# An attention and mixture-of-experts kernel whose setup is re-sorted around one batch, with later row sends and changed tail, projection and masks

## The chip, the cores and the metric

One core of a Trainium2 chip runs the whole kernel. The metric is device time in microseconds of one execution; lower is better.

## The reference

The input x is (8 batches, 512 tokens, 128). It is normalised over its last axis (xn), and two branches read xn. The first is causal attention with 32 query heads, 16 key and value heads of 64, an ALiBi bias, and an output projection. The second is a mixture of 8 experts: a gate chooses the best two of eight for each token, each expert is 128 to 512 to 128 with an exact GELU. The result is x plus attention times silu of the mixture.

```
qkv = xn @ W_qkv
scores = q @ k.T / 8 + slope[h] * (j - i);  causal;  softmax;  @ v;  @ W_out
gate_logits = xn @ gate_w + gate_b;  top 2;  softmax over the two
y[e] = gelu(xn @ w1[e] + b1[e]) @ w2[e] + b2[e];  weighted sum over the two
out = x + s * silu(ffn)
```

## The kernel before

All matrix work is done in fp16 pairs: a number is held as a high and a low half, and a product is three matmuls (`three`). The attention is cut into 64 **bodies**, each one pair of key and value heads (two slots) of one batch. A body consists of named steps: K, Q, V projections, M (rough scores, whose row peaks DVE takes as B), C (turned shifts), S (scores, ten groups), E (exponentials on ScalarE), L (low halves on POOL), P (values), N (normalise), A (output halves, moved through a transposing DMA), O (output projection, accumulated into `att` by DVE). `ORDER` writes out by hand, for each engine, the steps of one **window** in a fixed order; an entry such as `("R0", 2, 0)` is step R0 of the body two ahead of the window, at place 0 in per cent of the window. Engines run their lists strictly in order. Each half of the bodies has entering windows (before its first body), a loop over windows in pairs, some windows written out at either end, and leaving windows.

Around them: a **setup** (load x, statistics on DVE, normalised tiles in `mix`, turned by TensorE into `xT_hi` and `xT_lo`; weights split into halves; gate logits; the choice of two experts; ranks of the tokens; routing, which gives each token a slot in `slot_x`). Then the first half of the bodies. During it ScalarE (R), POOL (I, D) send each tile's rows to their slots with indirect DMAs, two transfers for each of 32 tiles, and the expert weights are loaded and split (W). Then the expert blocks. Then the second half, in which expert outputs are fetched and added into `mix` (F, G). Then the **tail**: silu, multiply, add x, write out.

Before the change the setup handles all eight batches at each step, the choice stands before the first projections, and POOL waits for the routing before it starts its windows. Row t is sent in step with body t. In a score group each part ends with its own mask matmul of 67 columns (line 887). The project step waits for both slots and goes through four token tiles with both slots inside. The tail is one silu over 4096 columns, four pieces of 1024 columns multiplied on DVE, and two of them added on POOL and two on DVE.

## Time and profile before

| what | us |
|---|---|
| median of three runs | 1264.25 (1263.28 to 1268.05) |
| profiled execution | 1263.92 |
| its span | 1262.0 |
| PE busy | 1154.3 (91%) |
| DVE busy | 1015.8 (80%) |
| ACT busy | 935.5 (74%) |
| POOL busy | 879.9 (70%) |

PE is TensorE, DVE VectorE, ACT ScalarE, POOL GpSimd. The span counts from the first to the last record of the profiled execution; 1.9 us lie around it. PE's matmuls are pipelined and their ends are modelled, so the distance between the starts of two of them says more than their lengths.

### The profile page before, as it was taken

To read this page: it belongs to the slowest core of one execution; us is meant where nothing else is said; L and a number is where in the kernel's file an instruction comes from. 1 tells how busy PE (TensorE), PEld (TensorE's weight loads), DVE (VectorE), ACT (ScalarE), POOL (GpSimd) and SP (SyncE) were. 2 spreads that over 40 slices of the span, in tenths; PEclk is the share of its full clock that TensorE was granted. 3 is DMA by queue.
4 is the path that set the end of the run, shared out by engine and by line. 5 is a ranking of instruction groups with operands and counts; after the bars stand their busy time and mean duration, and the time that the engine had idled before them with its cause. 6 is when DMAs were issued, how large, how long until landed. Compare 5 with 4: busy or idle time off the path is not lost.

```text
span 1262.0 us, 54043 instructions
## 1 busy us (share of the span) xinstructions
PE 1154.3 (91%) x17610; PEld 915.0 (73%) x17610; DVE 1015.8 (80%) x3107; ACT 935.5 (74%) x1790; POOL 879.9 (70%) x1088
## 2 busy tenths in 40 slices
PE   1449999999999999998999789999999999999992
PEld 0327777777777777787888658777777777777782
DVE  8758888888888888885777668888888888888874
ACT  1328888888888888886666468888888888888882
POOL 9128888888888888884000068888888888888883
PEclk9669999999999999999999989999999999999996
DMA  6416666666666666674333366665555555555553
GB/s 211 171 38 134 142 140 148 143 142 144 144 142 144 144 142 144 145 141 93 86 89 82 99 156 137 136 137 133 133 133 133 133 133 133 133 133 133 133 116 84
DMA packets 286165, 165.10 MB, mean 131 GB/s; under 512 B 175011, under 2 KB 274691, under 8 KB 285445
## 3 DMA queue, kind: packets, MB, share of 16 engines
q1 hardware_dynamic: 281988, 155.63, 53.9%
q0 software_dynamic: 4096, 8.40, 2.3%
q8 instruction: 51, 0.84, 0.3%
q14 instruction: 30, 0.24, 0.1%
HBM read 15.76 MB, written 16.78 MB: 26 GB/s over the span
## 4 chain that ended last, share of the span: by engine, by line
PE 78%; DVE 6%; DMA 4%; issue 4%; ACT 3%; SPq 2%; POOL 2%; ACTq 0%; POOLq 0%; DVEq 0%
PE ps L880 10%; PE ps L854 10%; PE ps L782 8%; PE ps L783 7%; PE ps L784 7%; PE ps L884 6%; PE outs L911 6%; PE outs L915 5%; PE outs L913 5%; PE ps L881 4%; DMA k_st<-stage 3%; PE ps L887 2%; PE ps L863 2%; ACT q_st L1109 2%; PE outs L783 1%
## 5 line engine op out<-in xcount | busy, mean ns | idle before, releaser
L743 POOL TENSOR_TENSOR t_lo<-stage 128x512 f16<-128x512 f32 x640 | 654.6, 1038 | 106.6 <-ACT stage L1120 102.1
L1302 DVE CUSTOM_DVE_ANT_0 stage<-ps,kmask 128x512 bf16<-128x512 f32 (+3 forms) x1024 | 467.1, 488 | 118.8 <-PE ps L854 101.6
L1120 ACT ACTIVATE stage<-ps,slope 128x512 f32<-128x512 f32 (+1 forms) x768 | 455.6, 619 | 120.0 <-PE ps L887 82.1
L880 PE MATMUL ps<-q_st,k_st 128*128 128x256 f16 (+3 forms) x1024 | 305.8, 301 | 10.5 <-ACT stage L1120 6.9
L911 PE MATMUL outs<-v_sp,stage 128*128 128x65 f16 x2560 | 282.1, 194 | 4.3 <-DVE stage L1332 2.8
L913 PE MATMUL outs<-v_sp,stage 128*128 128x64 f16 x2560 | 281.9, 193 | 0.0
L915 PE MATMUL outs<-v_sp,t_lo 128*128 128x65 f16 x2560 | 281.8, 193 | 0.0
L854 PE MATMUL ps<-k_st,stage 128*128 128x512 f16 (+3 forms) x1024 | 251.7, 302 | 12.8 <-DVE spread L1302 5.5
L911 PEld LDWEIGHTS outs<-v_sp,stage 128*128 128x128 bf16 x2560 | 238.4, 98 | 12.2 <-issue 4.4
L913 PEld LDWEIGHTS outs<-v_sp,stage 128*128 128x128 bf16 x2560 | 235.9, 98 | 9.0 <-issue 0.3
L915 PEld LDWEIGHTS outs<-v_sp,t_lo 128*128 128x128 f16 x2560 | 235.9, 98 | 0.0
L881 PE MATMUL ps<-q_st,k_st 128*128 128x128 f16 x1024 | 224.2, 219 | 0.0
L884 PE MATMUL ps<-q_st,k_st 67*128 67x384 f16 (+2 forms) x768 | 211.6, 276 | 0.0
L887 PE MATMUL ps<-late_q,late_k 66*128 66x67 f16 x1024 | 188.0, 195 | 0.0
L1109 ACT CAST q_st<-ps 1x512 f16<-1x512 f32 x256 | 147.6, 577 | 17.9 <-PE ps L863 12.3
L880 PEld LDWEIGHTS ps<-q_st,k_st 128*128 128x128 f16 x1024 | 100.2, 98 | 45.5 <-issue 21.6
L1077 ACT ACTIVATE stage<-ps,qscale 128x512 f16<-128x512 f32 x128 | 88.6, 692 | 48.7 <-PE ps L784 48.5
L704 POOL COPY slot_now<-slot_of 128x1 uint32 (+1 forms) x128 | 23.3, 183 | 141.4 <-DMA slot_y<-stage 141.4
L854 PEld LDWEIGHTS ps<-k_st,stage 128*128 128x128 f16 x1024 | 81.7, 98 | 49.3 <-issue 21.6
L884 PEld LDWEIGHTS ps<-q_st,k_st 67*128 67x128 f16 x768 | 74.9, 97 | 51.5 <-issue 1.6
L881 PEld LDWEIGHTS ps<-q_st,k_st 128*128 128x128 f16 x1024 | 100.3, 98 | 13.2 <-issue 0.9
L887 PEld LDWEIGHTS ps<-late_q,late_k 66*128 66x128 f16 x1024 | 100.8, 98 | 0.0
(199 smaller groups left out, 2731.6 us busy)
## 6 DMA issues: line engine op xcount, KB each, us to landing
k_st<-stage SPq DMA_DIRECT2D x256, 128.0 KB, 2.5
q_st<-stage SPq DMA_DIRECT2D x256, 128.0 KB, 2.4
q_st<-stage SPq DMA_DIRECT2D x256, 64.0 KB, 2.1
k_st<-stage SPq DMA_DIRECT2D x128, 64.0 KB, 2.1
slot_y<-stage SPq DMA_DIRECT2D x40, 128.0 KB, 2.0
X<-in_L_attn_inputs SPq DMA_DIRECT2D x8, 512.0 KB, 6.3
slot_x<-att SPq DMA_DIRECT2D x2, 2048.0 KB, 8.7
wx_raw<-in_L_ffn_w SPq DMA_DIRECT2D x64, 64.0 KB, 1.8
```

Source lines behind the costliest of these rows:

```text
L743: pool.tensor_tensor(t_lo[r], t_p[r], upper(t_p[r]), ALU.subtract).then_inc(s[f"lo{u % NG}"], 1)
L854: mm = pe.matmul(M_ps[h][:, c0:c0 + w], q_raw[sl][:, 0, i * P:(i + 1) * P], k_st[par][sl][:, 2 + h, 0:w], start=True, stop=True)
L880: pe.matmul(d, k[:, 0, at], q[:, 0, seen], start=True, stop=False, skip_group_check=True)
L881: pe.matmul(d[:, 0:P], k[:, 1, at], q[:, 1, at], start=False, stop=True, skip_group_check=True)
L884: pe.matmul(d[:, P:], k[far, 1, at], q[far, 1, (kt + 1) * P:SEQ], start=False, stop=True, skip_group_check=True)
L887: mm = pe.matmul(d[:, LATE:P], late_k[late, :], late_q[late, LATE:P], start=False, stop=True, skip_group_check=True)
L911: pe.matmul(d, p_hi, v[:, with_one], start=(opens and i == kt), stop=False, skip_group_check=True)
L913: pe.matmul(d[:, OUT_COL[sl]:OUT_COL[sl] + DH], p_hi, v[:, lo], start=False, stop=False, skip_group_check=True)
L915: mm = pe.matmul(d, t_lo[r][:, c], v[:, with_one], start=False, stop=(closes and i == QT - 1), skip_group_check=True)
L1109: ins = act.copy(q_st[sl][h][DH:DH + 1, 1, :], M_ps[0][SHIFT[h]:SHIFT[h] + 1, :])
L1120: e = act.activation(t_p[r][:, c0:c1], S_ps[u % 2][:, c0:c1], ACT.Exp, scale=slope[:, bass.ds(pair_index(n) * 2 * SLOTS + sl * 2 + h, 1)])
L1302: ins = dve.tensor_tensor_reduce(junk[h][:, c0:c0 + w], M_ps[h][:, c0:c0 + w], kmask[:, SEQ - w:SEQ], -1.0 / 1024, 3e38, ALU.add, ALU.min, ...
```

## The change

The setup starts with one batch of x, then the K and V weights, then Q, then the rest of x, then W_out (to another place). DVE, ScalarE and TensorE carry batch 0 through to the projections of body 0, with the splits of weights in between, and only then take batches 1 to 7, whose tiles are normalised half by DVE and half by ScalarE (`norm_odd`). POOL makes the mask rows first, and its share of the weight splits is gone. The gate follows, then the entering windows, and the choice of experts is cut into three parts that DVE runs after its steps B1, B3 and B5 of the first entering window (`CHOICE`). The ranks follow the entering windows on TensorE. POOL waits for the routing only before it sends the first row.

Rows are sent with the body two later (`sent_with`), R0 stands at place 72 and not 0 of ScalarE's list, and since 32 rows must still go in the first half, bodies 30 and 31 send two rows each. The loops end one pair of windows earlier, and those windows are written out.

In a score group one matmul masks all parts (its moving operand is repeated, its output lies in two places, 67 columns each). The project step goes slot by slot and waits for a slot just before it. The accumulation multiplies by 1/WS. The tail has three pieces of 14, 14 and 4 tiles, each with its own silu, multiplied and added on POOL, DVE and DVE; the first two start before the last body is complete.

```diff
-            ("R0", 2, 0), ("E0", 0, 4), ("E1", 0, 8), ("C1", 0, 12), ("E2", 0, 20), ("A1", -1, 26), ("E3", 0, 29),
...
+            ("E7", 0, 71), ("R0", 2, 72), ("A0", 0, 76), ("E8", 0, 79), ("W0", 0, 83), ("E9", 0, 89), ("Q0", 2, 94),
...
+                if "Y" in tasks and name in CHOICE:
+                    tasks["Y"](n, 0, CHOICE[name])
+
+
+        CHOICE = {"B1": 0, "B3": 1, "B5": 2}
...
-            start, end = lo + 2 * UNROLL, hi - UNROLL
+            start, end = lo + 2 * UNROLL, hi - 2 * UNROLL
...
+
+        LAST = NT - QT
+        PIECES = [(0, LAST // 2), (LAST // 2, LAST), (LAST, NT)]
+
         def out_chunk(v, c):
 
-            return v[:, 8 * c:8 * c + 8, :].rearrange("p t d -> p (t d)")
+            t0, t1 = PIECES[c]
+            return v[:, t0:t1, :].rearrange("p t d -> p (t d)")
+
+        def finish(eng, c):
+
+
+            need(eng, "silu", c + 1)
+            eng.wait_ge(s["acc"], BODIES if c == 2 else BODIES - PAIRS)
+            eng.wait_ge(s["xend"], 64)
+            a, g, xx = (out_chunk(v, c) for v in (att, mix, X))
+            eng.tensor_tensor(a, a, g, ALU.mult).then_inc(s[f"gated{c}"], 1)
+            eng.wait_ge(s[f"gated{c}"], 1)
+            eng.tensor_tensor(xx, xx, a, ALU.add).then_inc(s[f"fin{c}"], 1)
+
+        def sent_with(n):
+
+
+            if not isinstance(n, int):
+                return [n - UNROLL]
+            return [t for t in range(NT) if min(t + UNROLL, HALF - UNROLL + (t - NT) // 2 + UNROLL) == n]
...
+            inputs(0)
+            for c in (1, 0):
+                sp.dma_start(stage[:, c, :], w_qkv[:, c * CH:(c + 1) * CH]).then_inc(s[f"wq{c}"], 16)
+            for c in range(1, 4):
+                inputs(c)
...
-            sp.wait_ge(s["attz"], 1)
+            sp.wait_ge(s["rows"], ROW_STEPS)
...
-                                       row_now[par][:, 0:D], ALU.subtract).then_inc(s["ready0"], 1)
-                indices(n, k, par)
+                for i, t in enumerate(sent_with(n)):
+                    at = t % UNROLL if isinstance(t, int) else par
+                    if isinstance(t, int) and (t, k) == (0, 0):
+                        pool.wait_ge(s["routed"], 1)
+                        pool.wait_ge(s["zeros"], 16 * ZERO_DMAS)
+                    need(pool, f"sent{at}", t // UNROLL * 32)
+                    if k == 0:
+                        pool.wait_ge(s["rhi"], t + 1)
+                        pool.tensor_tensor(row_now[at][:, D:2 * D], mix[:, bass.ds(t, 1), :].rearrange("p a d -> p (a d)"),
+                                           row_now[at][:, 0:D], ALU.subtract).then_inc(s["ready0"], 1)
+                    indices(t, k, at)
...
+            finish(pool, 0)
...
-                    late = slice(0, P - LATE - 1)
-                    mm = pe.matmul(d[:, LATE:P], late_k[late, :], late_q[late, LATE:P],
-                                   start=False, stop=True, skip_group_check=True)
-                mm.then_inc(s[f"scored{u % NG}"], 1)
+
+                late, first = slice(0, P - LATE - 1), [c0 // P for _, _, c0 in GROUPS[u % NG]]
+                d = S_ps[u % 2].rearrange("p (t c) -> p t c", c=P)[:, first[0]:first[-1] + 1:max(first[-1], 1), LATE:P]
+                pe.matmul(d, late_k[late, :], late_q[late, LATE:P].unsqueeze(1).to_broadcast([P - LATE - 1, len(first), P - LATE]),
+                          start=False, stop=True, skip_group_check=True).then_inc(s[f"scored{u % NG}"], 1)
...
+                bank_free(n, "O0")
                 for sl in range(SLOTS):
                     need(pe, f"ta{sl}", (n + 1) * 16)
-                bank_free(n, "O0")
-                for t in range(QT):
-                    tok = slice(t * P, (t + 1) * P)
-                    for sl in range(SLOTS):
-                        j = bass.ds(pair_index(n) * SLOTS + sl, 1)
+                    j = bass.ds(pair_index(n) * SLOTS + sl, 1)
+                    for t in range(QT):
+                        tok = slice(t * P, (t + 1) * P)
+
                         mm = three(bank_of("O0")[:, tok], aT[par][sl][:, tok],
                                    aT[par][sl][:, (QT + t) * P:(QT + t + 1) * P],
                                    wo_hi[:, j, :].rearrange("p a d -> p (a d)"),
                                    wo_lo[:, j, :].rearrange("p a d -> p (a d)"),
...
+            turn_inputs(0)
+            bodies_of_half[:] = 0, HALF
+            keys(0, 0, 0)
+            vals(0, 0, 0)
+            queries(0, 0, 0)
+            queries(0, 0, 1)
+
+            pe.wait_ge(s["sm"], 80)
+            pe.transpose(ps[4][:, 0:E * FC], b1_in[:, :], ident[0:E * FC, 0:E * FC]).then_inc(s["b1tr"], 1)
+            for q in range(1, NB):
+                if q > 4:
+                    pe.wait_ge(s["xlo"], q - 3)
+                turn_inputs(q)
...
+            enter_bodies("PE", tasks, 0, HALF)
...
             pe.wait_ge(s["picked"], 1)
...
-            enter_bodies("PE", tasks, 0, HALF)
...
+                final = isinstance(n, int) and (n, sl) == (BODIES - 1, 1)
+                if final:
+                    act.wait_ge(s["added"], NT)
+                    for c in range(2):
+                        gates(c)
...
+                if final:
+                    gates(2)
...
+                for t in sent_with(n):
+                    at = t % UNROLL if isinstance(t, int) else par
+                    need(act, f"sent{at}", t // UNROLL * 32)
+                    act.copy(row_now[at][:, 0:D], mix[:, bass.ds(t, 1), :].rearrange("p a d -> p (a d)"))\
+                       .then_inc(s["rhi"], 1)
...
+            roots(0, 0, QT)
+            split_hi(K_PART)
+            split_hi(V_PART)
+            turned_hi(0)
+            split_hi(Q_PART)
+            bodies_of_half[:] = 0, HALF
+
+            act.wait_ge(s["wlo"], V_PART + 1)
+            k_hi_part(0, 0, 0)
+            v_hi_part(0, 0, 0)
             act.wait_ge(s["scales"], HQ)
-            act.wait_ge(s["wloP"], len(ON_POOL))
-            go_ahead("ACT", tasks, 0, HALF)
-            enter_bodies("ACT", {**tasks, "W": weights_hi, "R": send_hi}, 0, HALF)
+            for sl in range(SLOTS):
+                q_hi(0, 0, sl)
+            roots(1, QT, NT)
+            act.wait_ge(s["norm"], 1)
+            norm_odd(1)
+            for q in range(1, NB):
+                if q + 1 < NB:
+                    norm_odd(q + 1)
+                turned_hi(q)
+            split_hi(O_PART)
+            act.wait_ge(s["b1tr"], 1)
+            act.copy(b1T[:, :], ps[4][:, 0:E * FC]).then_inc(s["b1"], 1)
+            enter_bodies("ACT", tasks, 0, HALF)
+            act.wait_ge(s["gap"], 1)
+            act.activation(top[:, 5, :], top[:, 4, :], ACT.Exp).then_inc(s["topexp"], 1)
...
+            def choose(k):
+
+
+                if k == 0:
+                    dve.wait_ge(s["consts"], 9)
+                    dve.wait_ge(s["gate"], 1)
+                    small(dve.scalar_tensor_tensor(out=L, in0=ps[5][:, 0:NT * E].rearrange("p (t e) -> p t e", e=E),
+                                                   scalar=1.0 / WS, in1=gb[:, :].unsqueeze(1).to_broadcast([P, NT, E]),
+                                                   op0=ALU.mult, op1=ALU.add))
+                    pick(L, top[:, 0, :], top[:, 1, :], one1)
+                elif k == 1:
+                    small(dve.scalar_tensor_tensor(out=L2, in0=one1, scalar=-3e38, in1=L, op0=ALU.mult, op1=ALU.add))
+                    pick(L2, top[:, 2, :], top[:, 3, :], one2)
+                else:
+                    dve.tensor_tensor(top[:, 4, :], top[:, 2, :], top[:, 0, :], ALU.subtract).then_inc(s["gap"], 1)
+                    dve.tensor_tensor(chosen[:, 0:NT, :], one1, one2, ALU.add).then_inc(s["picked"], 1)
 
             def peaks(n, _, j):
...
 
+                if isinstance(n, int) and n == BODIES - 1:
+                    finish(dve, 1)
                 dve.wait_ge(s["op"], n + 1)
                 a = att[:, bass.ds(batch_index(n) * QT, QT), :].rearrange("p t d -> p (t d)")
-                dve.tensor_tensor(a, bank_of("O0")[:, :], a, ALU.add).then_inc(s["acc"], 1)
+                dve.scalar_tensor_tensor(out=a, in0=bank_of("O0")[:, :], scalar=1.0 / WS, in1=a, op0=ALU.mult,
+                                         op1=ALU.add).then_inc(s["acc"], 1)
...
+            statistics(0, QT)
+            scales_of(0, 0, QT)
+            norm_tiles(range(QT))
+            split_lo(K_PART)
+            turned_lo(0)
+            split_lo(V_PART)
+            bodies_of_half[:] = 0, HALF
+            statistics(QT, 2 * QT)
+            k_lo_part(0, 0, 0)
+            split_lo(Q_PART)
+            v_lo_part(0, 0, 0)
+            statistics(2 * QT, 4 * QT)
+            q_lo(0, 0, 0)
+            statistics(4 * QT, NT)
+            q_lo(0, 0, 1)
+            scales_of(1, QT, NT)
+            norm_tiles(range(QT, 2 * QT, 2))
+            for q in range(1, NB):
+                if q + 1 < NB:
+                    norm_tiles(range((q + 1) * QT, (q + 2) * QT, 2))
+                if q == 2:
...
+                turned_lo(q)
+            split_lo(O_PART)
...
+            enter_bodies("DVE", {**tasks, "Y": lambda n, _, k: choose(k)}, 0, HALF)
+            dve.wait_ge(s["topexp"], 1)
...
+            finish(dve, 2)
```

## Rows read from the trace of the kernel before

**Rows 1.** Windows: busy us of PE, PEld, DVE, ACT, POOL; granted clock, DMA share, GB/s

```profile
40.00:50.00 10.00, 4.91 (x131) 3.68 (x131) 8.68 (x10) 6.67 (x6) 4.15 (x2) 0.61 0.16 67
103.00:568.00 465.00, 460.93 (x7417) 367.73 (x7414) 400.46 (x1283) 390.23 (x747) 402.20 (x477) 1.00 0.64 144
1222.00:1262.00 40.00, 16.36 (x270) 14.63 (x268) 19.65 (x25) 14.16 (x20) 17.35 (x14) 0.69 0.34 80
```

**Rows 2.** Timeline of all engines, 85 to 92 us: start, length, engine, line, operation

```profile
85.24 0.97 POOL L721 DMA_INDIRECT slot_x<-row_now,slot_now  x1 [0.30 <-issue]
...
87.52 0.30 ACT L1142 CAST row_now<-mix 128x128 f16<-128x128 f32 x1 [11.98 <-DMA slot_x<-row_now,slot_now]
...
88.55 0.37 PE L880 MATMUL ps<-q_st,k_st 128*128 128x256 f16 x1 [4.86 <-ACT stage L1120]
```

**Rows 3.** Timeline of DVE, 0 to 115 us

```profile
10.54 1.65 DVE L1233 BATCH_NORM_STATS2 stats<-X 128x6 f32<-128x128 f32 x8 [0.23 <-DMA X<-in_L_attn_inputs]
...
41.66 2.29 DVE L419 SCALAR_TENSOR_TENSOR wq_lo<-stage,wq_hi 128x2048 f16<-128x2048 f32 x1 [1.12 <-ACT wq_hi L407]
...
45.85 0.41 DVE L1265 SCALAR_TENSOR_TENSOR wx_lo<-outs,gb 128x256 f32<-128x256 f32 x1
...
52.44 0.42 DVE L1285 TENSOR_TENSOR chosen<-wx_lo 128x256 f16<-128x256 f32 x1
...
53.65 0.69 DVE L1317 SCALAR_TENSOR_TENSOR stage<-ps,stage 128x512 f16<-128x512 f32 x1
...
63.98 0.69 DVE L1302 CUSTOM_DVE_ANT_0 stage<-ps,kmask 128x512 bf16<-128x512 f32 x1 [0.25 <-DVE wo_lo L419]
...
75.01 0.29 DVE L1367 TENSOR_TENSOR wx_lo<-outs,wx_lo 128x128 f32<-128x128 f32 x1
...
81.93 0.22 DVE L1399 TENSOR_TENSOR slot_of<-slot_of,slot_bits 128x64 uint32<-128x64 uint32 x1
```

**Rows 4.** Timeline of POOL, 0 to 32 us

```profile
21.49 3.54 POOL L681 MEMSET att<- 128x4096 f32 x1
...
29.55 2.11 POOL L700 TENSOR_TENSOR b_row<-wx_hi,b_row 1x1024 f16<-1x1024 f32 x1
```

**Rows 5.** Windows of the tile normalisation, L1248, alone: DVE busy us and count

```profile
22.00:25.00 3.00, 3.00 (x2) 1.00 0.00 0
31.70:33.00 1.30, 1.30 (x7) 1.00 0.94 403
```

**Rows 6.** Timeline of PE, 59 to 66 us: the matmuls of the ranks

```profile
60.18 3.31 PE L948 MATMUL outs<-chosen,ones 128*128 128x256 f16 x32
```

**Rows 7.** Timeline of all engines, 550 to 555 us, in window 29

```profile
551.72 0.59 ACT L1102 CAST stage<-outs 128x512 f16<-128x512 f32 x1
...
551.91 0.99 POOL L721 DMA_INDIRECT slot_x<-row_now,slot_now  x1 [0.17 <-issue]
...
552.97 0.69 DVE L1332 TENSOR_TENSOR stage<-outs,stage 128x512 f16<-128x512 f32 x1
...
553.11 0.22 PE L881 MATMUL ps<-q_st,k_st 128*128 128x128 f16 x1
...
553.16 0.20 PE L887 MATMUL ps<-late_q,late_k 66*128 66x67 f16 x1
...
553.20 0.38 PE L854 MATMUL ps<-k_st,stage 128*128 128x128 f16 x2
...
554.28 0.19 PE L911 MATMUL outs<-v_sp,stage 128*128 128x65 f16 x1
```

**Rows 8.** Timeline of all engines but PE, the last 25 us

```profile
1239.07 3.62 ACT L1213 ACTIVATE mix<-mix 128x4096 f32<-128x4096 f32 x1
...
1246.67 6.46 POOL L775 TENSOR_TENSOR X<-X,att 128x1024 f32<-128x1024 f32 x2 [12.62 <-DVE att L1443]
...
1250.97 3.25 DVE L1447 TENSOR_TENSOR X<-X,att 128x1024 f32<-128x1024 f32 x1
...
1255.39 1.22 DVE L1447 TENSOR_TENSOR X<-X,att 128x1024 f32<-128x1024 f32 x1
```

More of the change, by code:

```diff
@@ L551, in _ @@
             go_ahead("SP", stacks, 0, HALF)
+            sp.wait_ge(s["attz"], 1)
+            zx = slot_x.rearrange("(p a) d -> p (a d)", p=P)
+            none = att[:, :, :].rearrange("p t d -> p (t d)").bitcast(F16)
+            for c in range(0, ZERO, ZERO_ROW):
+                k = min(ZERO_ROW, ZERO - c)
+                sp.dma_start(zx[:, c:c + k], none[:, 0:k]).then_inc(s["zeros"], 16)
             enter_bodies("SP", {**stacks, "W": load_weights}, 0, HALF)
@@ L770, in _ @@
             leave_bodies("POOL", fetches, HALF, BODIES)
-            pool.wait_ge(s["xend"], 64)
-            for c in range(2):
-                pool.wait_ge(s["gated"], c + 1)
-                xx = out_chunk(X, c)
-                pool.tensor_tensor(xx, xx, out_chunk(att, c), ALU.add).then_inc(s["finP"], 1)
+            finish(pool, 0)
         @block.tensor
@@ L879, in scores @@
                     k, q = k_st[par][sl], q_st[sl][h]
-                    pe.matmul(d, k[:, 0, at], q[:, 0, seen], start=True, stop=False, skip_group_check=True)
+                    pe.matmul(d, k[:, 0, at], q[:, 0, seen], start=(c0 == 0), stop=False, skip_group_check=True)
                     pe.matmul(d[:, 0:P], k[:, 1, at], q[:, 1, at], start=False, stop=True, skip_group_check=True)
```

310 lines of the change are left out of this document (136 added, 174 removed), and 2 rows, old and new, of the table ORDER.

## The prediction, written before the change was run

> **What bounds the kernel now.** I read the busy times by stretch first, to see which stretches are not filled by TensorE. From 103 to 568 us PE is busy 460.93 of 465 us at a granted clock of 1.00, so that stage goes at PE's pace; the 40 us at the end hold only 16.36 us of PE work [rows 1]. The other open place is the start, so I read all engines around the first exponentials next. ScalarE sits idle 11.98 us until a transfer into slot_x lands, copies a row at 87.52, and only then starts the exponentials of body 0; TensorE's third score group, which needs one of them, starts at 88.55 after 4.86 us of idling [rows 2]. What holds that transfer is seen on DVE: the choice of experts from 45.85 to 52.86, the first projections of body 0 from 53.65, its peaks from 63.98, then the routing from 75.01 to 82.15, all in one queue [rows 3]. Everything before 88.55 is a serial prologue, everything after it runs at PE's pace. So moving that moment forward should shift the whole trace, until something in a PE-bound stage takes it back.
>
> **The setup.** It is a re-sorting of queues, so I add up the new queues. DVE first. Statistics of a tile cost 0.2 us (8 in 1.65) and splitting 2048 columns of weights 2.29 us [rows 3]; a 512-column low part 0.69 us [rows 3]. Up to the scales of batches 1 to 7 DVE has 32 statistics 6.6, aggregates about 2.2, two sets of seven short operations about 4.5, four normalised tiles 1.0, the splits of K, V and Q 4.6, five low parts 3.5, and some 1.5 us of waits on weights and on PE (an estimate): 24 us. The old one begins its statistics at about 5 us, so I take 28 to 29 us.
>
> Then come 14 tiles on DVE and 14 on ScalarE. POOL's big memset of att begins at 21.49 and its work on b2 ends at 31.66 [rows 4]; in 22 to 25 us DVE finished two tiles in 3 us, and from 31.7 on seven in 1.3 us [rows 5]. POOL's work is only permuted, so its end stays, and the tiles crawl until about 31.7. After that DVE needs 14 x 0.19 + 7 x 0.69 = 7.5 us, ScalarE somewhat more (two tiles and a 512-column cast per batch, about 1.3 us, 7 batches, of which one or two are done by then): the last low part at about 39.5 us. From 40 to 50 us PE ran 131 matmuls in 4.91 us [rows 1], the gate's 128 and three wide ones of about 0.5; the gate alone then 3.4: 43 us, only 3 us earlier than before.
>
> The gain is behind that. Old: choice 7.0, body 0's projections about 8 us (53 to 61), ranks 3.3, entering the bodies 11.0 (63.98 to 75.01), routing 7.1, first rows sent and waited for 5.4 us. New: entering and choice together, 11.0 + 6.1 - 0.6 (the choice's own 15 operations without the one that stood behind POOL, less what falls into DVE's wait for the shifts) = 16.5, to 60 us; three short operations and the ranks (3.31 us for 32 matmuls [rows 6], only behind the entering windows) to 62.3; routing 7.1 to 69.4; two peaks, the turned shifts, and the third score group at 71. The exponential of the gap needs a table load on ScalarE behind its last queries, at 59.5: hidden by the ranks, and worth 1.5 us if it isn't. The projections of body 0 now lie under the statistics and transfers; body 0's stacking waits for POOL's mask rows, due at 16, still 25 us ahead of use. The old moment is 88.55, so **-17.5 us**; bounds -22 (no crawling, no waits) and -11 (ScalarE paces the batches at 1.8 us and choice and peaks do not overlap). The three transfers that clear slot_x move behind body 0's stacking, are out by 29 us, land by about 42, and the first rows go after 69. TensorE's granted clock falls where the prologue leaves it idle (0.61 in 40 to 50 us [rows 1], so partly at the lower of its two levels), and will again; I count no difference.
>
> **Rows sent two bodies later.** Row t goes with body t+2, at the middle of ScalarE's window and no longer at its head; that removes the 11.98 us wait [rows 2], counted above. In the steady stage the copy (0.3 us) now stands ahead of the cast A0, at 551.72, which DVE follows at 552.97 to 553.66 and PE's values of the second slot at 554.28 [rows 7]: 0.62 us of slack, more than 0.3, so nothing. But in windows 28 and 29 two rows go each time, and here the copy in place 72 waits for sends that POOL issues in places 62 and 75 of the same window. A second send begins at 551.91 there, and one lands 2.26 us after it begins (85.24 to 87.5) [rows 2, 7]. In window 28 ScalarE would take row 29 at 536.6 + 2.3 (window 29's times less 15.3), 2.8 us late with the copy; less 0.6 slack 2.2 us. In window 29 both sends are double, the last begins near 554, lands at 556.2: 4.8 us late, less 0.6: 4.2 us. Queued behind the copy are A0, E8, E9 and Q0, and PE waits for A0 first. Sum **+6.4 us**; bounds 0 (if later slack takes it back) and +12 (if a landing takes about 5 us, twice the one seen).
>
> **Masks.** Per body 16 mask matmuls of 67 columns become 10, six of them of 134. One costs 0.04 us from its start to the next one's (553.16 to 553.20), a 128-column one 0.05 (553.11 to 553.16) [rows 7]; so 2 x 0.034 against 0.062, some 5 ns saved, times 6 times 64: **-2 us**; bounds 0 and -5. The Trainium skill, "TensorE: Matmul & The Clock Gate", Back-to-back issue gap, gives about 81 ns for a sustained matmul of 128 columns; by that a merged one would cost more than the two it replaces, about 12 ns x 384 = 5 us lost as an estimate. Row 553.11 shows 50 ns in this very stream, so the measurement decides and the sum stays without it; that a wide matmul of two pieces is slower than the row's by 20 ns, and gives +7 for the -2 us, has a chance of 0.02, inside rival 3's.
>
> **Projection.** Same 24 matmuls, ordered by slot; only at the very end does it matter, where half of them need not wait for the last transpose: 12 x 0.11 at the low clock, -1.3 us, in the tail below. The scaling by 1/WS goes from the end into the accumulation at the same length.
>
> **Tail.** Now: silu of 4096 columns 3.62 us after the last cast (hidden by the last transfer and projection), then DVE and POOL take turns: a 1024-column piece costs 1.22 us alone, yet 3.25 when POOL also has one, and POOL's two cost 6.46; DVE ends at 1256.6, 5.4 us before the end [rows 8]. That fits to the hundredth with whole instructions excluding each other: POOL's piece about 2.1, DVE's 1.22. New pieces: 1792 columns twice, 512 once. Two silus fill ScalarE's gap before the last cast (table 1.28 + 2 x 1.7 from 1232.8: to 1237.5, delaying it 0.3). POOL multiplies 1235.8 to 1239.5; DVE is free at 1239.5; then POOL 3.7 and DVE 2 x 2.13 take turns to 1247.5; last accumulation 0.7, last piece 2 x 0.7: 1249.6. Output transfers (2 MB from 1245.5 on, at some 270 GB/s, 7.7 us) then bind, not DVE: end at about 1255.5. **-6.5 us**; bounds -10 (DVE's end plus 2 less) and -3. The Trainium skill, "SBUF — State Buffer", two separate sides, states this exclusive lock of VectorE and GpSimd; the trace agrees, and I share nothing between them in the sum.
>
> **Sum.** -17.5 + 6.4 - 2 - 6.5 = -19.6, against the profiled execution's own 1263.92 (span 1262.0): 1244.3. The median, 1264.25, is 0.3 more: I say 1244.5.
>
> **Rivals.**
> 1. The doubled rows cost nothing: PE has other work before A0's values, or ScalarE catches up. Then 1238. For it: ScalarE is idle about 2 us per window. Against it: 0.62 us of slack in PE's strict order.
> 2. The setup gives less: the normalised tiles wait for POOL past 31.7, or choice and peaks alternate badly with PE, and the third score group comes at 77 or later. Then 1250 to 1252. For it: rows 5. It decides if the last low part comes after 45.
> 3. The copy in its new place delays every body of the first half, 28 x 0.3 = +8.4: 1253. Against it: the slack of 0.62.
> 4. Slower than before: the merged mask, with its repeated moving operand and its split output, streams at a quarter of the rate: 134 columns in 0.223 instead of 0.062, +0.16 x 384 = +62 us, 1306. It would make the change slower from about 0.12 us per merged matmul on (20 us / 384 = 52 ns over my 62). Against it: the rank matmuls also repeat their moving operand, and 32 of 132 columns on the mean took 3.31 us, 103 ns each, which is one column a cycle at the low clock [rows 6].
>
> **Chances.** My forecast, 1240 to 1249: 0.56. Rival 1, 1234 to 1240: 0.20. Rival 2: 0.13. Rival 3: 0.06. Rival 4: 0.03; another loss, 0.02. The range reaches from rival 1 to the first of rival 2: 1235 to 1252. 0.5% is 6.3 us, about what a measurement of this kernel can tell from no change. Faster by more than that: 0.95; within: 0.02; slower: 0.03.
>
> **What would show it.** The first exponential near 62 and the third score group (88.55 now) near 71; PE at 1.00 by 85; ScalarE's idle ahead of the row copies in windows 28 and 29, 3 and 5 us, with PE waiting for DVE's low part after it; 640 mask matmuls of 67 or 134 columns; POOL and DVE in turns from 1216 on, with the end 6 us after the last accumulation. Wrong I am if the batches wait on ScalarE or POOL past 45 us, if the routing starts after 66, or if bodies between 100 and 500 us take other than 15.5 us each.

## The result, and the profile after

The changed kernel took 1253.15 us (median of 4 runs, 1251.98 to 1254.56) against 1265.18 for the kernel before on the same chip: ratio 0.9911, 95% interval 0.9883 to 0.9939. So it is faster, by less than forecast, and 1253.15 is just above the range of 1235 to 1252. Measured again on another chip it was 1260.51 against 1268.13, ratio 0.9948 (0.9935 to 0.996); the two intervals barely overlap, so by the two ratios the gain is 0.5 to 0.9%. The profiled execution shows a span of 1251.1 us against 1262.0.

The clearest ruler is the first exponential (E0) of each body: its time after less its time before is how far ahead the changed kernel is. It reads -12.1 at the third score group of body 0 (78.10 for 90.20), -14.4 to -14.7 from body 5 to body 27, -14.9 at body 28, -3.3 at the first matmul of the expert stage (582.81 for 586.11), -0.2 at body 32, -3.8 at the last exponential, and -10.9 at the end. So almost all of the setup's gain is gone by the middle, and most of the final gain is made behind it.

Windows of the kernel after, with the columns of [rows 1]: the end of the setup, the stage at TensorE's pace, the tail.

```profile
40.00:50.00 10.00, 7.19 (x141) 4.64 (x139) 6.96 (x14) 3.38 (x5) 0.00 (x0) 1.00 0.26 107
88.00:550.00 462.00, 452.78 (x7064) 359.68 (x7063) 391.66 (x1260) 380.45 (x733) 397.44 (x477) 0.99 0.63 143
1211.00:1251.00 40.00, 22.18 (x377) 18.75 (x376) 23.81 (x42) 19.80 (x32) 27.10 (x20) 0.82 0.43 104
```

The middle stage now has over 9 us without a matmul and a clock of 0.99, where [rows 1] had 4 us and 1.00. DVE of the kernel after in its setup, against [rows 3]:

```profile
26.20 0.90 DVE L1328 TENSOR_SCALAR rs<-mv 128x28 f32<-128x28 f32 x1
...
28.25 1.07 DVE L1332 TENSOR_TENSOR rs<-rs 128x28 f32<-128x28 f32 x1
...
29.57 1.99 DVE L1334 TENSOR_TENSOR rs<-rs 128x28 f32<-128x28 f32 x1
...
42.41 0.69 DVE L1349 TENSOR_TENSOR xT_lo<-ps,xT_hi 128x512 f16<-128x512 f32 x1 [0.56 <-ACT xT_hi L1112]
...
47.39 0.69 DVE L1392 CUSTOM_DVE_ANT_0 stage<-ps,kmask 128x512 bf16<-128x512 f32 x1 [0.88 <-PE ps L878]
...
56.56 0.42 DVE L1380 TENSOR_TENSOR chosen<-wx_lo 128x256 f16<-128x256 f32 x1
...
66.57 0.29 DVE L1487 TENSOR_TENSOR wx_lo<-outs,wx_lo 128x128 f32<-128x128 f32 x1 [0.72 <-PE outs L994]
...
67.93 1.02 DVE L1494 TENSOR_SCALAR per_e<-per_e 128x8 f32<-128x8 f32 x1
68.99 1.28 DVE L1497 TENSOR_TENSOR wx_lo<-wx_lo,per_e 128x320 f32<-128x320 f32 x1
...
75.14 0.23 DVE L1519 TENSOR_TENSOR slot_of<-slot_of,slot_bits 128x64 uint32<-128x64 uint32 x1
```

The three scale operations at the top work on 28 columns and take 0.90 to 1.99 us; their neighbours of the same size take 0.18 to 0.46. All the while POOL is on one partition of b2, the second bias of the experts (the last row of [rows 4] as well), and each of the three ends 0.03 to 0.05 us behind one of its operations. The last low part ends at 43.1, the first peak is at 47.39, the choice ends at 56.98, the routing runs from 66.57 to 75.4, with two short operations held to over 1 us again. POOL of the kernel after:

```profile
21.45 3.52 POOL L712 MEMSET att<- 128x4096 f32 x1
24.93 1.04 POOL L728 TENSOR_SCALAR wx_hi<-wx_hi 1x1024 f32<-1x1024 f32 x1
26.04 1.03 POOL L729 CAST b_row<-wx_hi 1x1024 f16<-1x1024 f32 x1
27.15 1.04 POOL L728 TENSOR_SCALAR wx_hi<-wx_hi 1x1024 f32<-1x1024 f32 x1
28.25 1.03 POOL L729 CAST b_row<-wx_hi 1x1024 f16<-1x1024 f32 x1
29.36 2.15 POOL L731 TENSOR_TENSOR b_row<-wx_hi,b_row 1x1024 f16<-1x1024 f32 x1
```

**The doubled rows.** Timelines of ScalarE, DVE and TensorE in bodies 28 and 29, two of the first and one each of the others, against [rows 7]:

```profile
524.59 0.30 ACT L1204 CAST row_now<-mix 128x128 f16<-128x128 f32 x1 [2.74 <-DMA slot_x<-row_now,slot_now]
...
544.88 0.30 ACT L1204 CAST row_now<-mix 128x128 f16<-128x128 f32 x1 [4.25 <-DMA slot_x<-row_now,slot_now]
```

```profile
546.62 0.69 DVE L1422 TENSOR_TENSOR stage<-outs,stage 128x512 f16<-128x512 f32 x1 [4.78 <-ACT stage L1160]
```

```profile
526.25 0.19 PE L936 MATMUL outs<-v_sp,stage 128*128 128x65 f16 x1 [1.99 <-DVE stage L1422]
...
547.46 0.22 PE L936 MATMUL outs<-v_sp,stage 128*128 128x65 f16 x1 [4.24 <-DVE stage L1422]
```

One reads the chain backwards: TensorE waits for DVE's low part, DVE for ScalarE's cast, which stands behind the row copy, which waits for a transfer. Bodies 28 and 29 are 18.4 and 21.4 us for 15.4 and 15.2. But two waits of 6.2 us don't make the 9.2 us by which these two are longer. Windows of body 29, before and then after:

```profile
540.66:555.87 15.21, 15.21 (x250) 12.31 (x249) 13.43 (x43) 12.86 (x24) 13.38 (x17) 1.00 0.64 146
```

```profile
528.77:550.17 21.40, 17.16 (x245) 13.46 (x244) 13.29 (x43) 13.38 (x26) 16.31 (x22) 0.90 0.54 112
```

TensorE's busy time for about as many matmuls rose from 15.21 to 17.16, at a granted clock of 0.90 on the mean (0.66 in the 5 us behind the wait): part of the stretch is at the lower of the two levels. The spacing says the same: behind the wait of body 29 the matmuls of 64 and 65 columns start 0.055 us apart (547.48 to 548.74, 23 of them), and later 0.03 us (550.74 to 551.10, 12 of them). In body 28 the busy time rose from 15.38 to 16.39, at 0.94. That is 3 us more, and with the 6.2 of waits it makes the 9.2.

**The tail.** POOL, DVE and the output transfers, one timeline, against [rows 8]:

```profile
1232.11 4.00 POOL L459 TENSOR_TENSOR att<-att,mix 128x1792 f32<-128x1792 f32 x1 [1.83 <-ACT mix L1146]
...
1235.33 2.66 DVE L459 TENSOR_TENSOR att<-att,mix 128x1792 f32<-128x1792 f32 x1
1236.19 5.62 POOL L461 TENSOR_TENSOR X<-X,att 128x1792 f32<-128x1792 f32 x1
1238.03 5.67 DVE L461 TENSOR_TENSOR X<-X,att 128x1792 f32<-128x1792 f32 x1
1241.83 5.01 SPq L631 DMA_DIRECT2D out_x<-X  x3
...
1245.11 0.69 DVE L461 TENSOR_TENSOR X<-X,att 128x512 f32<-128x512 f32 x1
```

DVE ends at 1245.8 and the span 5.3 us later. From the last exponential to the end it is 22.7 us for 29.9 before.

### The profile page after: what moved, and what is told of

Its sections match the earlier page's. It is cut to its first block and busy times, and to the rows that moved or that the text cites. A ratio compares the mean times of both kernels' runs of the same rounds, so it can differ in the third digit from the quotient of the medians.

```text
span 1251.1 us, 52908 instructions
## 1 busy us (share of the span) xinstructions
PE 1154.0 (92%) x17226; PEld 912.5 (73%) x17226; DVE 1005.5 (80%) x3099; ACT 939.0 (75%) x1807; POOL 878.3 (70%) x1086
## 3 DMA queue, kind: packets, MB, share of 16 engines
HBM read 15.76 MB, written 16.78 MB: 26 GB/s over the span
## 5 line engine op out<-in xcount | busy, mean ns | idle before, releaser
L904 PE MATMUL ps<-q_st,k_st 128*128 128x256 f16 (+3 forms) x1024 | 302.5, 301 | 4.0 <-DMA k_st<-stage 1.8
L878 PE MATMUL ps<-k_st,stage 128*128 128x512 f16 (+3 forms) x1024 | 252.8, 304 | 14.9 <-DVE spread L1392 7.6
L913 PE MATMUL ps<-late_q,late_k 66*128 66x134 f16 (+1 forms) x640 | 136.0, 212 | 0.0
L878 PEld LDWEIGHTS ps<-k_st,stage 128*128 128x128 f16 x1024 | 84.3, 98 | 53.0 <-issue 24.3
L905 PEld LDWEIGHTS ps<-q_st,k_st 128*128 128x128 f16 x1024 | 100.4, 98 | 17.2 <-issue 0.6
L1422 DVE TENSOR_TENSOR stage<-outs,stage 128x512 f16<-128x512 f32 x128 | 88.0, 687 | 21.7 <-ACT stage L1160 21.7
```

Of the source, the lines that this page charges most:

```text
L878: mm = pe.matmul(M_ps[h][:, c0:c0 + w], q_raw[sl][:, 0, i * P:(i + 1) * P], k_st[par][sl][:, 2 + h, 0:w], start=True, stop=True)
L904: pe.matmul(d, k[:, 0, at], q[:, 0, seen], start=(c0 == 0), stop=False, skip_group_check=True)
L905: pe.matmul(d[:, 0:P], k[:, 1, at], q[:, 1, at], start=False, stop=True, skip_group_check=True)
L913: pe.matmul(d, late_k[late, :], late_q[late, LATE:P].unsqueeze(1).to_broadcast([P - LATE - 1, len(first), P - LATE]), start=False, stop=Tr ...
```

## The experiments

Each ratio is to the kernel before, on the same chip. "Stretch 31 to 32" is the time from E0 of body 31 to E0 of body 32; it holds the expert stage, and was 157.8 before and 162.9 after.

| kernel | ratio (95% interval) | bodies 28, 29, 30 | stretch 31 to 32 | E0 of body 32 |
|---|---|---|---|---|
| after, first profile | 0.9911 (0.9883 to 0.9939) | 18.4, 21.4, 15.2 | 162.9 | 728.2 |
| after, again | 0.9948 (0.9935 to 0.9960) | 17.6, 22.3, 16.5 | 161.3 | 727.8 |
| four buffers | 0.9874 (0.9855 to 0.9892) | 15.3, 16.3, 18.0 | 161.8 | 721.8 |
| doubled first, shared wait | 0.9894 (0.9878 to 0.9910) | 15.2, 15.3, 15.1 | 161.3 | 727.8 |
| b2 behind the choice | 0.9902 (0.9887 to 0.9917) | 17.9, 21.1, 16.5 | 162.5 | 724.2 |
| four buffers and b2 | 0.9854 (0.9837 to 0.9872) | 15.3, 18.0, 16.2 | 161.8 | 718.2 |
| doubled first, own waits, b2 | 0.9854 (0.9834 to 0.9874) | 15.3, 15.3, 15.0 | 160.0 | 719.4 |

**Four buffers** in the doubled bodies:

```diff
-        row_now = [... for par in range(2)]
+        row_now = [... for par in range(4)]
+        def row_buffer(t):
+            return {29: 2, 30: 1, 31: 3}.get(t, t % UNROLL)
```

> The changed kernel with four row buffers in place of two, so that in bodies 28 to 31 no doubled copy of ScalarE waits for the sends of a row two earlier. Theory A (the two doubled bodies cost what ScalarE waits for a buffer): bodies 28 and 29, 18.4 and 21.4 us after the change, come back to about 15.4 each, and the total falls by about 9 us, to some 1244 us; the 2.5 us of the last windows of the half, where POOL's doubled sends stand ahead of its low parts, stay. Theory B (the price is POOL's doubled work itself, its sends and subtractions ahead of the low parts of the exponentials): bodies 28 and 29 keep most of their length and the total stays within 3 us of 1253.

The copies of ScalarE no longer wait for a transfer (both pairs stand without idle time, at 521.54 and 537.21), and by body 31 the kernel is 5.4 us ahead of the changed one, 6.4 by body 32. That is less than the 9 of theory A, as what is lost is now spread over bodies 29 and 30. Who makes TensorE wait between 510 and 577 us is another engine; its waits in the kernel with four buffers:

```profile
PE outs L944 <- POOL t_lo L789: 5.3, 9, 1.1
```

Nine waits for POOL's low parts, none over 1.1 us. In the changed kernel, up to its first matmul of the expert stage (510 to 582.8), these were 2.9 us, beside 6.8 for DVE. So both theories hold a part: some 6 us were the buffers, and the rest, which the waits put down to POOL, fits its doubled sends. The granted clock is 1.00 in each of bodies 28, 29 and 30 here.

**Rows only** (the kernel before, with rows two bodies later alone):

> The kernel before with one part of the change alone: rows are sent two bodies later, doubled in the last four bodies of the half. Setup, projection, masks and tail stay as before. Theory A: body 0 no longer waits for the routing ahead of its first copy, so its exponentials begin 5 to 12 us sooner, of which the third score group, that wants the keys of the setup, gives back a part; from body 28 on 11 us are lost and in the expert stage up to 3. Sum: 1262 to 1270 us, no gain from this part by itself. Theory B (the forecast's term: the doubled rows cost 6.4 us): bodies 28 and 29 are 3.2 us longer each and the time is 1258 to 1262 us.

Ratio 1.0087 (1.0069 to 1.0106), 1280.0 us: slower. E0 of body 5 came 4.7 us sooner; bodies 28 to 30 took 18.7, 21.6 and 16.5, so body 31 began 6.9 us later than before. From body 28 to 31 that is 11.4 us lost, for 9.6 and 10.9 in the two profiles of the changed kernel. The total is worse than either theory's: from E0 of body 32 to the last exponential it takes 7.5 us more than before (511.8 for 504.3; bodies 38 to 58 are 15.94 us for 15.80). The kernel before has no trace from this chip, so whether the rows or the chip lengthen them stays open. This part loses by itself; it pays only as what makes the setup's re-sorting possible.

**Doubled first.** Rows 0 and 1 with body 2, rows 2 and 3 with body 3, then one each:

```diff
-            return [t for t in range(NT) if min(t + UNROLL, HALF - UNROLL + (t - NT) // 2 + UNROLL) == n]
+            return {2: [0, 1], 3: [2, 3]}.get(n, [n] if n > 3 else [])
```

> The changed kernel with the doubled rows at the beginning of the half: rows 0 and 1 go with body 2, rows 2 and 3 with body 3, from there row n with body n, each of the four first rows in a buffer of its own, so that nothing in it waits for an earlier row's send. Theory A (11.4 us are lost to doubling at the end of the half, with two buffers): all of it comes back but what two more copies of 1.3 us and two more pairs of sends cost in bodies 2 and 3, about 1 to 2 us, and the time is 1241 to 1244 us. Theory B (doubling costs the same wherever it stands): bodies 2 and 3 are 3 to 6 us longer each, and the time stays at 1250 to 1254 us. If the 3 us at the end of the expert stage come from rows that land late, they come back as well (1239).

Body 2 took 23.5 us, body 3 17.1: 9.3 over the changed kernel's, so neither theory's number for the bodies. My edit was at fault for part of it: rows 0 and 2 counted on one semaphore, so ScalarE's copy of row 4 waited 4.21 us for row 2's transfers, though its buffer had long been free. So I gave each buffer its own (with b2 behind the choice as well):

> The changed kernel with the second bias behind the choice and the doubled rows at the beginning of the half (rows 0 and 1 with body 2, rows 2 and 3 with body 3), this time with a semaphore for each of the four buffers, so that row 4 waits for row 0 alone. Theory A (what is left of the doubling is POOL's and ScalarE's doubled work, about 2 us per doubled body wherever it stands): bodies 2 and 3 together 4 to 6 us longer than 31.3, no loss at the end of the half, and the total within 1.5 us of the one with four buffers at the end, a ratio of 0.985. Theory B (at the beginning the doubling lies in idle time of the pipeline): 1 us, and a ratio of 0.981 to 0.982. Theory C (as in the earlier kernel that doubled first, 10 us): 0.989.

Bodies 2 and 3 took 20.1 and 17.2: 6.0 us over 31.2, inside theory A. What is left is TensorE waiting 4.2 us for POOL's low parts and a clock of 0.91 in body 2. From body 28 to the first matmul of the expert stage it takes 61.0 us, before 60.8, with four buffers 66.3 and in the changed kernel 72.4. So the work of doubling costs 6.0 us at the beginning and 5.5 at the end, and what the changed kernel lost beyond that went with the two buffers.

**The second bias behind the choice:**

```diff
             pool.wait_ge(s["consts"], 9)
+            pool.wait_ge(s["picked"], 1)
             b2v =
```

> The changed kernel with one more wait on POOL: its work on the second bias (which ran until 31.5 us and beside which VectorE's scale operations took 0.9 to 2.0 us) starts when the choice of experts is made. Theory A (that work held VectorE's scale operations, and the gate and the choice stand behind them): the last scale operation ends near 28 instead of 31.8, the low parts at about 40 instead of 43.1, the first exponential of body 0 about 3 us sooner, and the time is 1249 to 1250.5 us. Theory B (the entry is bounded by ScalarE's and VectorE's own evictions of the turned inputs, which are as many as before): the first exponential moves by under 1 us and the time stays within 1 us of 1253. A third way: the work on the second bias now stands in POOL's row ahead of its low parts of body 0 and costs there what it gave before.

DVE's scale operations in that kernel, the same three as above:

```profile
26.23 0.18 DVE L1329 TENSOR_SCALAR rs<-mv 128x28 f32<-128x28 f32 x1
...
27.28 0.19 DVE L1333 TENSOR_TENSOR rs<-rs 128x28 f32<-128x28 f32 x1
...
27.72 0.19 DVE L1335 TENSOR_TENSOR rs<-rs 128x28 f32<-128x28 f32 x1
```

0.90, 1.07 and 1.99 us became 0.18, 0.19 and 0.19 with nothing changed but what POOL does beside them. The Trainium skill, "SBUF — State Buffer", two separate sides, states such an exclusive lock of VectorE and GpSimd; the trace agrees, on a single partition too. In that kernel the last low part ends at 39.5, E0 of body 0 comes at 63.41 for 67.05, and the 3.6 us are kept to the expert stage. That is theory A by the trace. Its total is not: 1249 to 1250.5 us would be a ratio of 0.987 to 0.988, and it is 0.9902 (0.9887 to 0.9917). The ratios without the edit (0.9911 and 0.9948) lie so far apart that they cannot tell a step of this size.

**The changed kernel again, and both gains together:**

> The changed kernel as it is, once more, so that it shares a chip and the runs of the kernel before with the three below. Its ratio to before was 0.991 with an interval of 0.988 to 0.994; every theory expects that again. Of its trace the theories expect first exponentials at the same offsets from the kernel before: body 0 at about 67, body 28 to body 31 growing from 510 to 565, and 161 to 163 us from the first exponential of body 31 to that of body 32.

> The changed kernel with both edits that gained by themselves: four row buffers in the doubled bodies, and POOL's work on the second bias behind the choice of experts. By their first traces the one brought the first exponential of body 32 in 6.4 us sooner, the other 4.1 us. Theory A (they are independent, one in setup and one at the end of the half): together about 10 us less than the changed kernel on this chip, a ratio to before of about 0.983. Theory B (one hides the other, as POOL is the engine that both touch): 5 to 7 us less.

1249.30 us for 1260.51 on that chip: 11 us less, and E0 of body 32 comes 9.6 us sooner, where the two alone gave 6.4 and 4.1. So by the traces the two gains add up, though the ratio is 0.9854 and not the 0.983 of theory A, and its interval meets that of four buffers alone. Bodies of the second half took 15.80 us in both, though 15.65 in the changed kernel's first profile. It is not shown that the chip makes this difference: two further kernels below, alike in the second half and both measured on chip 13 but not in the same set of runs, took 15.65 and 15.81.

**Masks, projection, and the lost time in the expert stage.**

> The kernel before with the merged masks alone: one matmul for the two late masks of a score group in place of two. The forecast put this part at 2 us saved with bounds of 0 and 5. Theory A (TensorE is not what a body waits for): bodies of both halves keep their length within 0.02 us on the same chip, and the time is within 0.3% of before. Theory B (the second half's 0.1 to 0.2 us per body that the changed kernel saved is the masks'): bodies 38 to 58 are 0.1 us shorter each and the time 3 us less. If the merged matmul also decides how the last fetched rows of the expert stage arrive, 161 to 163 us stand between the first exponentials of bodies 31 and 32 in place of 157.8.

> The kernel before with the merged masks and with the new order of the projection's matmuls (by slot, each slot waiting for its own turned attention). Theory A (the projection's order is what shortens a body of the second half): against the kernel with the masks alone bodies 38 to 58 are 0.1 to 0.2 us shorter each, 3 to 4 us in all over both halves. Theory B: no difference, and the saving belongs to the rows or to setup. The 3 to 5 us lost between the first exponentials of bodies 31 and 32 are looked for here as well: 157.8 us if they belong to another part of the change.

> The kernel before as it is, for a trace on another chip than its first: its bodies of the second half were 15.80 us on the first chip, the changed kernel's 15.65 there and 15.80 on another. Theory A (the projection and the masks shorten a body of the second half by 0.13 us, and chips differ by as much): where this chip is the slower kind, the bodies of the kernel before are 15.93 to 15.95 us here, as the kernel with the rows alone showed. Theory B (nothing in the change shortens them, only the chip did): 15.80. From the first exponential of body 31 to that of body 32 both expect 157.8 us, and TensorE's 16 KB fetch of instructions some 2.7 us ahead of the last transposing fetch of rows.

Ratios 0.9977 (0.9964 to 0.9990), 0.9960 (0.9944 to 0.9976), 1.0001. Bodies of the first half keep their length (15.54 to 15.55). Bodies 38 to 58 took 15.84 with the masks and 15.76 with both, on one chip; on another 15.79 before and 15.74 with the masks. Only pairs of one set of runs are compared here. Over 32 bodies that is 1.6 us for the masks and 2.4 for the projection, together 4.0 for the 3.6 that the changed kernel gained in its second half. And the masks alone bring the stretch 31 to 32 to 161.6, where the kernel before has 157.8 and 159.0 and the rows alone 158.1. What comes in late is the last fetch of rows through the transposing DMA: SyncE's issue, TensorE's wait, and the DMA of TensorE's instructions in that time (queue q8), for the masks alone:

```profile
705.54 2.64 SPq L560 DMA_TRANSPOSE xg_more<-slot_x  x1
```

```profile
710.36 0.39 PE L782 MATMUL ps<-xg_more,wx_hi 128*128 128x256 f16 x1 [3.27 <-ACT X L1174]
```

```profile
q8 instruction: 1, 0.02, 2.2%
```

The rows land at 709.76 here. The last 0.6 us of TensorE's wait go to ScalarE (`<-ACT X`), which had itself idled 4.65 us until a transfer of expert outputs landed. Before, the issue took 1.26 us, the wait 2.30, and no packet of q8 is in it:

```profile
706.19 1.26 SPq L560 DMA_TRANSPOSE xg_more<-slot_x  x1
```

```profile
709.64 0.28 PE L782 MATMUL ps<-xg_more,wx_hi 128*128 128x256 f16 x1 [2.30 <-DMA xg_more<-slot_x]
```

The two kernels differ in TensorE's program alone, and q8's packets stand elsewhere in the whole stage: 3 us later behind the loop with the masks. So I take q8 for TensorE's. Fewer mask matmuls make its program shorter and move the places where its next 16 KB are fetched. To move them back I put empty instructions at its beginning, where it idles until 9.26 us in the changed kernel and 16.93 in the kernel before. The first way (plain ones) left none in the program, and q8's packets stood where they had stood:

> The kernel before with the merged masks, and 96 empty instructions on TensorE at its very beginning, where it idles for over 9 us: as many instructions as the merged masks take out of its program ahead of the expert stage (48 matmuls of two instructions). Theory A: the masks cost nothing there by themselves; they move the place at which the next 16 KB of TensorE's program are fetched into the last transposing fetch of rows, which lands 1.2 to 1.7 us later for it, and the clock goes down in the longer idle time. With the 96 back, the fetch of instructions is 2.7 us ahead of it again, TensorE's idle time there 2.3 us in place of 3.3, and 158 us stand between the first exponentials of bodies 31 and 32 in place of 161.6: 3.5 us off the total. Theory B (the merged matmul itself, or chance of the chip): 161.6 us as with the masks alone.

> The changed kernel with four row buffers and the second bias behind the choice, and 96 empty instructions on TensorE ahead of its first wait. Theory A (place of the instruction fetch): the 16 KB fetch, which came 0.02 us after the last transposing fetch of rows was issued, now comes about 3.3 us ahead of it (96 of 256 instructions of a block that lasts 8.7 us), and the stretch from the first exponential of body 31 to that of body 32 falls from 161.8 to 158 to 159 us; the total is 3 to 4 us less than without them, a ratio to before of about 0.982 or 0.983 against 0.985. Theory B: 161.8 us again and no change.

> As the one before with 192 empty instructions in place of 96, as a control of the place: the fetch of instructions that was at the last transposing fetch comes about 6.5 us ahead of it, and the next one 2 us behind its issue, before it has landed. Theory A: a collision again, or half of one, 160 to 162 us between the first exponentials of bodies 31 and 32, wherever the records show the 16 KB packet inside the 3.3 us of the transposing fetch, and 158 to 159 where they show it outside. Theory C (any empty instructions help, for another reason): as good as 96.

Stretches 161.3, 162.8 and 162.5; ratios 0.9985, 0.9842 and 0.9850. They tell nothing of the fetch. The last two kernels are the same program as the one with four buffers and b2, so with the 0.9854 above there are three measurements of it. With a wait on each the empty instructions stay:

```diff
+            for _ in range(96):
+                pe.wait_ge(s["ident"], 1)
+                pe.nop(nofuse=True)
```

> The kernel before with the merged masks, and at TensorE's beginning 96 empty instructions that each carry a wait (for the identity, long fulfilled after the first), so that they stay in the program. In the run before this one the 96 had left none, and TensorE's fetches stood where they stood without. Theory A (place of the fetch): the 16 KB fetches after the loop go back from 8.5 to about 11.8 us ahead of body 31's first exponential, the one near the last transposing fetch of rows comes 2 to 3 us ahead of it, TensorE idles 2.3 us there in place of 3.3, and 158 to 159 us stand between the first exponentials of bodies 31 and 32 in place of 161.6. Theory B (the merged matmul itself): the fetch moves and the 161.6 us stay.

> The changed kernel with four row buffers and the second bias behind the choice, and the same 96 empty instructions with waits at TensorE's beginning. Theory A: TensorE's fetch that stood 0.02 us behind the issue of the last transposing fetch moves some 3 us ahead of it, its idle time there goes from 3.0 to 2.3 us, the stretch from 161.8 to 158 to 159 us, and the ratio to before from 0.985 to 0.982. The price at the beginning is under 1 us, if the 96 pass while TensorE waits for VectorE's first tiles (until 9.26 us). Theory B: the stretch stays at 161.8 us.

> The one before with the 96 empty instructions with waits as well. Theory A of the fetch: 3 us less than without them, by a stretch of 158 to 159 us between the first exponentials of bodies 31 and 32. Theory B: the same time as without.

The packet moved to 2.7, 3.2 and 2.7 us ahead of the issue. The issue took 1.27 us each time, for 2.64, 2.05 and 2.56 without the 96, and the landing 3.3, 3.5 and 3.3 for 4.2, 4.1 and 4.7. TensorE waited 2.30, 3.00 and 2.29 us, for 3.27, 3.02 and 3.54. The masks with 96 real ones:

```profile
706.20 1.27 SPq L560 DMA_TRANSPOSE xg_more<-slot_x  x1
```

```profile
709.68 0.28 PE L782 MATMUL ps<-xg_more,wx_hi 128*128 128x256 f16 x1 [2.30 <-DMA xg_more<-slot_x]
```

So it is shown that the fetch of instructions delays the landing; all 18 traces fit. In eleven the packet starts up to 0.6 us behind the issue; there the issue takes 2.05 to 2.64 us and the landing 3.8 to 4.8. In six no packet starts between issue and landing, and it is 1.26 to 1.27 and 3.3 to 3.5 us. In the one with masks and projection the packet starts 2.87 us behind the issue: 1.27 and 5.05 us. TensorE got about 1 us of it back in two of the three kernels and nothing in the second, where the rows were also asked for later (137.59 us behind E0 of body 31, for 136.67).

The stretches were 161.3, 161.3 and 158.5: for the first two theory B's number, for the third theory A's. The ratios 0.9986 (0.9973 to 0.9998), 0.9843 (0.9822 to 0.9863) and 0.9860 (0.9839 to 0.9881) are none apart from its like without the 96. In the last two kernels that says little, for there the 96 have a price at the beginning, where under 1 us was expected. TensorE's first matmul of the last one:

```profile
12.05 1.09 PE L834 MATMUL outs<-ident,mix 128*128 128x128 f32 x4 [12.05 <-issue]
```

It waits for nothing but the instructions ahead of it; without the 96 it starts at 9.30. E0 of body 31 comes 1.65 us later in that kernel (561.07 for 559.42), which takes back the 1.5 us that its stretch is shorter (158.5 for 160.0). With the masks alone the 96 pass in idle time (16.96 for 16.93), and there the stretch stays at 161.3. So the collision is not all of the 3 us. Nor do the ratios of the masks alone show such a loss: all three are below 1, and their profiled executions were each the slowest of ten, 1.5 to 2.8 us above the median. How much of it an ordinary run of that kernel has is not known; the changed kernel's profiled execution lies at its median. In the traces the rest stands behind that wait. Windows from the matmul that ends the wait to E0 of body 32: the kernel before, the changed kernel, the masks alone, the masks with 96:

```profile
709.64:728.47 18.83, 13.94 (x123) 9.69 (x123) 10.39 (x30) 7.66 (x17) 1.75 (x4) 0.82 0.23 69
707.39:728.24 20.85, 15.77 (x123) 11.45 (x124) 11.04 (x32) 7.74 (x17) 1.67 (x4) 0.67 0.20 60
710.36:731.84 21.48, 16.38 (x122) 11.99 (x123) 11.03 (x31) 8.13 (x18) 1.75 (x4) 0.66 0.22 66
709.68:730.60 20.92, 15.82 (x122) 11.60 (x123) 10.47 (x30) 7.67 (x16) 1.75 (x4) 0.67 0.21 64
```

In the changed kernel 1.05 us are lost between the first matmul of the expert stage and this one (124.58 us for 123.53) and 2.0 behind it. Of the 2.0, 1.8 are busy time of TensorE, for as many matmuls at a clock of 0.67 in place of 0.82. With the 96 the clock is as low, though the wait is the short one; and the kernel before, in its second trace, has 19.55 us and 0.74 there. What sets the clock in this piece stays open.

## Why the prediction failed

**The sum by its steps.** Setup -14.4 to -14.9, forecast -17.5. Rows two bodies later +11.6, forecast +6.4. Expert stage +3.1, not in the forecast. Second half -3.6, forecast -2 for the masks over both halves. Tail -7.1, forecast -6.5. Together -14.9 + 11.6 + 3.1 - 3.6 - 7.1 = -10.9 for -19.6.

**The step that failed is the price of the doubled rows**, +6.4 in the sum and +11.6 measured. Its mechanism was right, nearly to the number: TensorE's waits were forecast at 2.2 and 4.2 us in the two bodies and were 1.99 and 4.24, and behind the copy stood what I had named. What the sum had at nothing are two things: the lower clock behind each wait (3 us, as TensorE's busy time shows), and POOL's doubled sends ahead of its low parts, which go on into body 31 (17.43 us from its E0 to the first matmul of the expert stage for 15.39, and 16.79 in the changed kernel's second profile; with the doubling moved to the beginning it is 15.44). I had put +12 at a slow landing; the bound held, for another reason.

**Setup.** Entering and choice together took from 47.39 to 63.9, 16.5 us, as forecast. The 3.6 us too late come from one step: "the tiles crawl until about 31.7. After that 7.5 us". It was not the tiles that crawled but the scales ahead of them, so no batch was done by then, and the low parts ended at 43.1 for 39.5. The 7.5 us, which are DVE's work alone, were short as well: the seven batches took 11.4 us (31.7 to 43.1), of which ScalarE was busy 10.0, and just as long with b2 behind the choice (28.1 to 39.5), where POOL did nothing beside them. My lower bound had ScalarE set the pace here; the sum had not. The forecast had seen POOL hold DVE [rows 5]; it did not ask which of DVE's operations would now lie under POOL's. The routing lost another 1.7 us (8.8 for 7.1) in the same manner, beside POOL's low parts, now that body 0 runs beside it. Body 4, which took 16.9 us before and 15.4 after, gave 1.5 us back. That is not the setup's: it takes 15.4 to 15.5 with the masks alone and with the rows alone too, and 16.2 in the second trace of the kernel before.

**The rest.** The copy in place 72 costs next to nothing in the steady stage (rival 3 fell: bodies 8 to 26 take 15.54 us on the mean for 15.55 before, and 15.58 with the rows alone, on another chip). Rival 4 fell too: a merged mask matmul of 134 columns takes 0.06 us from its start to the next one's (550.68 to 550.74), as forecast, and by the bodies the masks save 1.6 us in the second half. The forecast was 2 for both halves, and the three ratios with the masks alone say the same: 0.9977, 0.9985 and 0.9986, 1.8 to 2.9 us less. The order of the projection was priced in the tail only and saves 2.4 us in the second half. Of rival 2 half came true: the third score group began at 76.66 for its 77, as POOL did hold VectorE until 31.6 us, but the last low part ended before its 45. The measured 1253 is rival 3's number, and that is chance, as its delay did not occur. In the tail silu, POOL and DVE went as forecast, 3.7 to 3.8 us earlier throughout; DVE ended at 1245.8 and the transfers 5.3 us after it. The clock at the end of the expert stage was in no rival.

**The best version** has four row buffers and the second bias behind the choice (the doubling at the beginning with own waits is as good): ratio 0.9854, in two more measurements 0.9842 and 0.9850. By the first it is 6 to 9 thousandths better than the changed kernel, and 19 us less than the kernel before on its chip.

## What to carry to other kernels

A wait of TensorE, where it sets the pace, can cost more than its length: here two waits of 2.0 and 4.2 us cost 9.2, by the lower clock behind them, while nine waits of at most 1.1 us left the clock at 1.00. When work is doubled to catch up, count its buffers: two buffers for two rows a body make the copies wait for transfers just begun. And when a queue is re-sorted, ask for each short operation of VectorE what POOL does at that moment, even if it works on one partition only.

## What the hardware showed that I had not expected

- A VectorE operation of 28 columns took 1.99 us beside a POOL operation on a single partition, and 0.19 without it.
- One 16 KB fetch of TensorE's instructions just behind the issue of a transposing fetch of rows made that land in 3.8 to 4.8 us for 3.3 to 3.5, and the issue of it take 2.1 to 2.6 us for 1.3. Where it falls depends on the length of TensorE's program ahead of it.
- The same body of the second half took 15.65 us in one profile of a kernel and 15.80 in another, with the first half's bodies equal to 0.01 us. Why is open.
